# Routing of the first half in three pieces behind the last groups, and two splits of the shared expert moved ahead

## The chip, the core and the metric

One Trainium2 chip; the kernel runs on one of its cores. The metric is the device time of one execution in microseconds (us). Engines are TensorE (PE; PEld for its weight loads), VectorE (DVE), ScalarE (ACT), GpSimd (POOL) and SyncE (SP), which issues DMAs.

## The reference

x has 4096 rows of 128 values. Four sub-layers are applied one after the other, each to the layer norm of x, and each result is added to x:

```python
x = x + attn_a(layernorm(x))   # scores against 512 keys, (1 - arccos(s)/pi)**9, values, l2 norm
x = x + ffn(layernorm(x))      # layer 0 of the experts
x = x + attn_b(layernorm(x))   # linear attention, elu features, 16 heads
x = x + ffn(layernorm(x))      # layer 1 of the experts, same weights

# ffn
logits = xf @ gate_w + gate_b
top_w, top_i = top_k(logits, 2)
gw = softmax(top_w)
for e in range(8):
    h = gelu(xf @ w1[e] + b1[e])
    out = out + combine[:, e:e+1] * (h @ w2[e] + b2[e])
shared = gelu(xf @ ws1 + bs1) @ ws2 + bs2
```

## The kernel before

**Tiling.** The 4096 rows are 32 tiles of 128 rows, in NG = 8 groups of TPG = 4 tiles. A half is 4 groups (HT = 16 tiles). The routed experts work on units of 256 rows (39 of them per layer), the shared expert on NA = 16 half groups n (two for each group).

**Layer 0, first part.** Attention a ends with the value products. The parts of each engine are laid out by `by_units` (line 150), a list of (lag, part): at step n a part works on half group or group n - lag. On VectorE the list (line 1888) holds `third`, `ninth` (the ninth power), `first_add` (adds the values to x, and the moments of the gate's norm), `first_shift`, `first_hi` and `gate_lo` (the rows in two f16 halves) and `gate_logits`. TensorE's list is FIRST_ORDER (line 111): turn the gate rows, `value(g)` (line 1098), gate products. GpSimd computes one power per group for the values' norm (`x_scale`) and one for the gate's norm (`group_root`, recorded at line 671). ScalarE makes the squares of the values, the angles, the normalised rows and copies of turned rows.

**Layer 1, first part.** Linear attention. The lists are laid out by `straight` (line 97): LIN_ORDER (line 105) for TensorE, lists of their own on VectorE (line 1885) and ScalarE. `lin_add` (line 1636 in the trace) adds the projected result, then moments; `gate_shift` makes the shift of the gate's norm; `gate_lo` and `gate_logits` follow at lags 3 and 4.

**Routing.** `routing(half)` (line 1683) takes a half's logits on VectorE through 17 numbered steps: the two largest of 8 with their experts (lines 1703 to 1716, ending in PM, the mask of both), gates from a Tanh that ScalarE makes in `gap(half)` (GW, CB, lines 1719 to 1723), and places: TensorE counts with two products in `route(half)` (line 1219), and VectorE adds a scan over tiles (lines 1729 to 1756, ending in SLF, the row's place). `rows(g)` (line 1762) copies a group's rows, destinations, gates and places into one of 4 buffers (slot g % 4; it waits until the scatters of group g - 4 have landed). `gate_parts(half)` (line 1775) splits the gates in bf16 terms.

The first half's routing stands inside `gate_logits` right behind the logits of group 3:

```python
                    if g == NG // 2 - 1:
                        routing(0)
                        rows(0)
                    if NG // 2 <= g < NG - 1:
                        rows(g - NG // 2 + 1)
```

and on TensorE `route(0)` stands ahead of `value(NG - 1)` and of `lin_project(NG // 2 + 1)`.

**Scatters.** `scatter(g, ...)` (line 717, recorded at line 724) on GpSimd writes a group's rows to DRAM by place, 8 indirect DMAs a group, 64 a layer. In layer 0 the first group's 4 + 4 stand between the last powers, in layer 1 groups 0 and 1 (16) do. The others follow in `paced(g)` (line 736), each group behind a signal:

```python
                behind = {2: gates_done, 3: routing_done, 4: summed(1), 5: summed(2), 6: summed(4), 7: summed(5)}
```

**Shared expert.** TensorE's `shared_up` (n = 0 to 3 early), ScalarE's `shared_gelu`, VectorE's `shared_split` (lines 1808, 1810; splits the Gelu into f16 halves), TensorE's `shared_down` (ending in line 1270) and `shared_turn`, ScalarE's copy (line 1015), VectorE's `shared_add`. In VectorE's loop `later_rows` puts rows(5), (6), (7) ahead of the splits 1, 3, 6, `later_gates` gate_parts(1) at 4, and `later_table` the table of units behind split 7.

**Routed experts.** SyncE waits for the table, stores padding rows, waits for the first four groups' scatters, issues six transposing loads (line 561), then waits for all rows (`all_rows_stored`, line 546); tail loads (line 568, gate and destination of a unit's rows) come only behind that. TensorE multiplies up and down, VectorE splits (lines 1901, 1904) and makes the output (line 1915, `routed_out`, line 1907), ScalarE takes Gelu (line 1026) and the low part (line 1036, `routed_low`, line 1030, which needs the unit's tail), GpSimd scatters the results (line 778). Six units are in flight.

**PSUM.** Three rings of two banks, A, B and C, with counted turns (`USES`, LIN_RING, `lin_turns`, `route_bank`, line 393).

## Time and profile before

| what | us |
|---|---|
| median of 3 runs | 698.61 |
| lowest and highest | 694.57, 699.79 |
| profiled execution | 695.24 |
| its span | 693.4 |
| DVE busy | 552.1 (80%) |
| PE busy | 497.8 (72%) |
| ACT busy | 465.5 (67%) |
| POOL busy | 375.5 (54%) |

Positions such as "at 272.77" are microseconds from the start of the span. A timeline row has start, duration, engine, line, operation and tiles; in square brackets stands how long the engine was idle before it and what released it. "issue" means that the engine waited for nothing that the profile shows. An indirect DMA's row on POOL is the time in which GpSimd makes it; its landing comes later.

### The profile page before, as it was taken

How to read it: one execution, taken by the hardware profiler on the slowest of the kernel's cores; microseconds unless marked ns; L12 is line 12 of the kernel's file. 1: busy time of each engine (PE TensorE's matmuls, PEld its weight loads, DVE VectorE, ACT ScalarE, POOL GpSimd, SP SyncE). 2: the span in 40 equal slices, each digit the busy share in tenths (PEclk: the TensorE clock that was granted, in tenths of full speed). 3: DMA queues.
4: the chain of work that ended last, by engine and by line, in shares of the span. 5: the costliest groups of instructions: out<-in, count | busy, mean ns of one | idle time of the engine just before them, and what ended most of it. 6: DMA issues, size and time to landing. Idle time of an engine off the chain costs nothing.

```text
span 693.4 us, 14048 instructions
## 1 busy us (share of the span) xinstructions
PE 497.8 (72%) x3817; PEld 360.3 (52%) x3818; DVE 552.1 (80%) x1229; ACT 465.5 (67%) x937; POOL 375.5 (54%) x382
## 2 busy tenths in 40 slices
PE   1276725655456998999977678757569999999760
PEld 1132305555422446787866466646224469888650
DVE  4989666978668985899989778786679859998991
ACT  1379988998234665989966767845535569999750
POOL 5032201323477776677757722226677737777773
PEclk9999977968558999999999999967689999999996
DMA  8700000000011144444473310001111444545943
GB/s 277 215 8 0 1 0 0 1 1 0 16 47 47 52 115 81 91 98 100 104 194 85 96 35 1 1 9 36 39 48 57 115 80 94 100 101 137 228 112 125
DMA packets 95054, 51.12 MB, mean 74 GB/s; under 512 B 76026, under 2 KB 84180, under 8 KB 94996
## 3 DMA queue, kind: packets, MB, share of 16 engines
q1 hardware_dynamic: 85908, 31.67, 20.5%
q0 software_dynamic: 9088, 18.76, 9.0%
q8 instruction: 25, 0.41, 0.2%
q14 instruction: 33, 0.27, 0.1%
HBM read 16.27 MB, written 23.90 MB: 58 GB/s over the span
## 4 chain that ended last, share of the span: by engine, by line
PE 27%; DVE 21%; issue 17%; ACT 13%; POOL 11%; SPq 8%; DMA 3%; DVEq 0%; POOLq 0%; ACTq 0%
POOL routed_rows L724 8%; SPq L561 5%; PE PC L1107 5%; PE PC L1314 4%; DVE big L1901 2%; DMA RR<-expert_results 2%; DVE RR L1915 2%; ACT SC L834 2%; SPq L568 2%; ACT big L934 2%; PE PA L1125 2%; DVE big L1539 2%; PE PC L1316 2%; PE PA L1296 1%; PE PA L1298 1%
## 5 line engine op out<-in xcount | busy, mean ns | idle before, releaser
L778 POOL DMA_INDIRECT expert_results<-RR,DG x156 | 171.1, 1097 | 73.0 <-issue 45.9
L724 POOL DMA_INDIRECT routed_rows<-big,SLQ x128 | 137.5, 1074 | 56.1 <-issue 45.0
L1314 PE MATMUL PC<-W,big 128*128 x624 | 117.4, 275 | 25.9 <-DVE RR L1915 24.7
L1026 ACT ACTIVATE SC<-PA,B1T,scl 128x256 f32<-128x256 f32 x208 | 100.5, 571 | 21.6 <-PE PA L1298 12.2
L1904 DVE SCALAR_TENSOR_TENSOR big<-SC,scl,big 128x1024 f16<-128x1024 f32 x78 | 100.3, 1286 | 2.8
L1316 PE MATMUL PC<-W,big 128*128 x468 | 86.5, 221 | 0.0
L1314 PEld LDWEIGHTS PC<-W,big 128*128 128x128 f16 x624 | 57.9, 98 | 41.5 <-issue 36.8
L1107 PE MATMUL PC<-QW,big 128*128 128x128 f32 x256 | 42.7, 345 | 42.8 <-DVE big L1539 28.1
L1901 DVE TENSOR_SCALAR big<-SC,scl 128x1024 f16<-128x1024 f32 x78 | 65.1, 835 | 5.8 <-ACT SC L1026 5.8
L671 POOL TENSOR_TENSOR RS<-VA,halfneg 128x4 f32<-128x4 f32 x24 | 28.4, 1185 | 67.9 <-DVE VA L1573 67.8
L1107 PEld LDWEIGHTS PC<-QW,big 128*128 128x128 f32 x256 | 41.2, 257 | 45.0 <-DVE big L1539 29.4
L1036 ACT ACTIVATE big<-PC,DG 128x128 f32<-128x128 f32 x156 | 50.0, 386 | 18.3 <-PE PC L1314 13.9
L1296 PE MATMUL PA<-big,W1H 128*128 128x256 f16 x208 | 56.9, 274 | 1.0 <-DMA big<-routed_rows 0.7
L1026 ACT ACTIVATE SC<-PB,B1T,scl 128x256 f32<-128x256 f32 x104 | 50.6, 580 | 10.1 <-DVE big L1904 7.2
L1297 PE MATMUL PA<-big,W1H 128*128 128x256 f16 x208 | 56.9, 273 | 0.0
L1298 PE MATMUL PA<-big,W1L 128*128 128x256 f16 x208 | 56.8, 273 | 0.0
L903 ACT ACTIVATE SC<-PA,B1T,scl 128x512 f32<-128x512 f32 x64 | 45.8, 773 | 12.8 <-PE PA L1213 11.2
L1915 DVE SCALAR_TENSOR_TENSOR RR<-PC,DG,big 128x128 f32<-128x128 f32 x156 | 47.0, 344 | 8.8 <-ACT big L1036 8.0
L1316 PEld LDWEIGHTS PC<-W,big 128*128 128x128 f16 x468 | 46.0, 98 | 1.3
L1810 DVE SCALAR_TENSOR_TENSOR big<-SC,scl,big 128x1024 f16<-128x1024 f32 x32 | 41.1, 1285 | 1.1
L1086 PE MATMUL PA<-QT,KT 128*128 128x512 f32 x64 | 32.9, 638 | 12.7 <-DVE QT L1399 12.1
L1015 ACT ACTIVATE big<-PC,scl 128x512 f32<-128x512 f32 x16 | 11.0, 687 | 41.3 <-PE PC L1270 41.3
(284 smaller groups left out, 1268.3 us busy)
## 6 DMA issues: line engine op xcount, KB each, us to landing
RR<-expert_results SPq DMA_DIRECT2D x16, 512.0 KB, 4.2
routed_rows<-pad_zeros SPq DMA_DIRECT2D x23, 128.0 KB
expert_results<-RR,DG POOLq DMA_INDIRECT x156
X<-n_L_attn_a_hidden_states SPq DMA_DIRECT2D x2, 1024.0 KB, 6.5
big<-in_L_ffn_w SPq DMA_DIRECT2D x1, 2048.0 KB, 9.0
routed_rows<-big,SLQ POOLq DMA_INDIRECT x128, 2.4
out_x<-X SPq DMA_DIRECT2D x8, 256.0 KB
big<-routed_rows SPq DMA_TRANSPOSE x78
```

The source lines that it names most:

```text
L724: pool.indirect_dma_start(routed, bass.IndirectOffsetOnAxis(ap=SLQ[:, slot, t, c:c + 1], axis=0), XHL[:, slot, t, c, :].bitcast(I32), None ...
L778: pool.indirect_dma_start(results, bass.IndirectOffsetOnAxis(ap=DG[:, k, r, 0:1], axis=0), YT[:, k, r, :], None).then_inc(result_stored[k] ...
L1026: ins = act.activation(HF[:, k % 3, b * RU:(b + 1) * RU], up_out(k, b), ACT.Gelu, scale=INV1, bias=B1T[:, bass.ds(b1_at + b, 1)])
L1107: last = pe.matmul(PC[slot][:, t * D:(t + 1) * D], powers, QW[:, b, :], start=(b == 0), stop=(b == HB - 1))
L1296: pe.matmul(o, W1H[:, at], xh, start=True, stop=False)
L1297: pe.matmul(o, W1H[:, at], xl, start=False, stop=False)
L1298: last = pe.matmul(o, W1L[:, at], xh, start=False, stop=True)
L1314: last = pe.matmul(both, hh, W2[:, :, at], start=(b == 0), stop=(b == HB - 1))
L1316: pe.matmul(both[:, 0, :], hl, W2H[:, at], start=False, stop=False)
L1901: dve.tensor_scalar(HH3[:, k % 3, :], HF[:, k % 3, 0:HB * RU], SH, None, ALU.mult).then_inc(s["rhh_ready"], 1)
L1904: dve.scalar_tensor_tensor(HL3[:, k % 3, :], HF[:, k % 3, 0:HB * RU], SH, HH3[:, k % 3, :], ALU.mult, ALU.subtract).then_inc(s["rhl_ready" ...
L1915: ins = dve.scalar_tensor_tensor(YT[:, k, r, :], down_out(k)[:, r, 0, :], DG[:, k, r, 1:2].bitcast(F32), LOW[:, k % 2, r, :], ALU.mult, AL ...
```

## The change

The routing of a half is cut in three functions with the same instructions in another order: `choose(half)` (11 steps, to PM), `place(half)` (the places, to SLF) and `gates(half)` (GW, CB). Layer 0 places them at the ends of steps 16, 17 and 18 of VectorE's list, with rows(0) behind the gates, rows(1) and rows(2) two and four steps on, and gate_parts(0) behind rows(2). Layer 1 has `choose` at the end of step 8, `place` between the add and the shift of group 7 in step 9, gates and rows(0) at the end of step 9, and rows(1), rows(2) and gate_parts(0) in step 10. TensorE's `route(0)` stands behind the last values and the last projection, in layer 1 in ring A instead of C. GpSimd's scatters all stand behind the last root. For the second half, VectorE does `choose(1)`, the splits 0 and 1 of the shared expert, `place(1)`, `gates(1)`, rows(3) and rows(4). ScalarE makes `gap(1)` between the Gelus 1 and 2; in layer 1 `gap(0)` moves to step 9.

```diff
 def lin_turns(groups):
...
-                if (what, n - lag) == ("project", groups // 2 + 1):
+                t.take(what, n - lag, LIN_RING[what])
+                if (what, n - lag) == ("project", groups - 1):
                     for slot in range(2):
-                        t.take("route", slot, "C")
-                t.take(what, n - lag, LIN_RING[what])
+                        t.take("route", slot, LIN_RING["route"])
...
             if half == 0:
-                return PC[slot], c_read[slot], lin_free("route", slot)
+                return PA[slot], a_read[slot], lin_free("route", slot)
...
                 if layer:
 
-                    for n in range(NG):
-                        if n >= 2:
+                    for n in range(2, NG + 2):
+                        if n < NG:
                             group_root(n, 2)
-                        if n >= 2:
-                            if n == NG - 1:
-                                scatter(0, 0, 0, range(2))
-                            group_root(n - 2, 3)
-                    scatter(0, 0, 0, range(2, TPG))
-                    group_root(NG - 2, 3)
-                    scatter(1, 0, 1, range(2))
-                    group_root(NG - 1, 3)
-                    scatter(1, 0, 1, range(2, TPG))
-                    for g in range(2, NG):
-                        paced(g)
+                        group_root(n - 2, 3)
                 else:
-                    for g in range(NG - 2):
+                    for g in range(NG):
                         x_scale(g)
                         group_root(g, 1)
-                    x_scale(NG - 2)
-                    scatter(0, 0, 0, range(2))
-                    group_root(NG - 2, 1)
-                    x_scale(NG - 1)
-                    scatter(0, 0, 0, range(2, TPG))
-                    group_root(NG - 1, 1)
-                    scatter(1, 0, 1)
-                    for g in range(2, NG):
-                        paced(g)
+                for g in range(NG):
+                    paced(g)
...
                 def first_gap(g):
-                    if g == NG - 1:
+                    if g == 0:
                         gap(0)
...
-                                  (1, lin_exp_q), (0, first_gap), (0, lin_normalise), (0, lin_turn_x),
+                                  (1, lin_exp_q), (NG + 1, first_gap), (0, lin_normalise), (0, lin_turn_x),
...
-                gap(1)
                 for n in range(EARLY):
+                    if n == 2:
+                        gap(1)
                     shared_gelu(n, 0, n, early=True)
...
                 def gate_logits(g):
                     logits(g, g // 2, g % 2, "")
-                    if g == NG // 2 - 1:
-                        routing(0)
+
+                def first_routing(n):
+
+                    if n == 0:
+                        choose(0)
+                    if n == 1:
+                        place(0)
+                    if n == 2:
+                        gates(0)
                         rows(0)
-                    if NG // 2 <= g < NG - 1:
-                        rows(g - NG // 2 + 1)
+                    if n in (4, 6):
+                        rows(n // 2 - 1)
+                    if n == 6:
+                        gate_parts(0)
...
                 if layer:
                     straight(NG, [(0, lin_combine), (1, lin_elu_k), (4, gate_logits), (0, lin_shift), (3, gate_lo),
-                                  (1, lin_mask), (1, lin_elu_q), (2, lin_add), (1, lin_divide), (2, gate_shift)])
+                                  (NG + 2, lin_rows), (1, lin_mask), (1, lin_elu_q), (2, lin_add),
+                                  (NG + 1, lin_place), (1, lin_divide), (2, gate_shift), (NG, lin_choose),
+                                  (NG + 1, lin_gates)])
                 else:
                     by_units(NG, [(6, first_hi), (0, third, 1), (6, gate_lo), (4, first_shift), (8, gate_logits),
-                                  (1, ninth, 1), (3, first_add)])
-                routing(1)
+                                  (1, ninth, 1), (3, first_add), (2 * NG, first_routing, 1)])
+                choose(1)
+                wait(dve, s["rhl_ready"], layer * UNITS)
+                for n in range(2):
+                    shared_split(n, 0, n, early=True)
+                place(1)
+                gates(1)
+                rows(3)
                 rows(4)
-                gate_parts(0)
-                wait(dve, s["rhl_ready"], layer * UNITS)
```

## Rows read from the trace of the kernel before

**Rows 1.** The page, part 4: the chain that ended last, shares by line.

```profile
POOL routed_rows L724 8%; SPq L561 5%; PE PC L1107 5%; PE PC L1314 4%; DVE big L1901 2%; DMA RR<-expert_results 2%; DVE RR L1915 2%; ACT SC L834 2%; SPq L568 2%; ACT big L934 2%; PE PA L1125 2%; DVE big L1539 2%; PE PC L1316 2%; PE PA L1296 1%; PE PA L1298 1%
```

**Rows 2.** The chain that ended last, 270 to 279 us: start, us, what.

```profile
272.77 2.35 DMA routed_rows<-big,SLQ
...
275.37 0.42 SPq L568
...
277.74 0.42 SPq L568
```

**Rows 3.** Timeline of GpSimd (POOL), layer 0: start, us, instruction, idle before.

```profile
179.08 1.30 POOL L724 DMA_INDIRECT routed_rows<-big,SLQ  x1 [8.12 <-issue]
...
196.41 1.04 POOL L724 DMA_INDIRECT routed_rows<-big,SLQ  x1 [0.19 <-issue]
...
217.74 1.02 POOL L724 DMA_INDIRECT routed_rows<-big,SLQ  x1 [0.30 <-issue]
```

**Rows 4.** Timeline of GpSimd, layer 1.

```profile
495.29 1.00 POOL L724 DMA_INDIRECT routed_rows<-big,SLQ  x1 [1.55 <-PE PC L1196]
...
560.84 0.95 POOL L724 DMA_INDIRECT routed_rows<-big,SLQ  x1 [0.30 <-issue]
```

**Rows 5.** Busy us by engine in a stretch; then PE clock, DMA share, GB/s.

```profile
580.00:590.00 10.00, 10.00 (x110) 9.10 (x106) 9.86 (x17) 9.44 (x24) 7.55 (x9) 1.00 0.46 98
```

**Rows 6.** Timeline of VectorE (DVE), layer 0.

```profile
169.40 0.29 DVE L1703 TENSOR_REDUCE MX<-big 128x16 f32<-128x128 f32 x1
...
173.05 0.29 DVE L1716 TENSOR_TENSOR PM<-big 128x128 bf16<-128x128 f32 x1
...
174.40 0.17 DVE L1729 COPY D<-region_of 128x8 f32<-128x8 f32 x1
...
177.90 0.17 DVE L1772 CAST SLQ<-SLF 128x8 uint32<-128x8 f32 x1
...
189.97 1.13 DVE L1547 SCALAR_TENSOR_TENSOR X<-PC,RX,X 128x128 f32<-128x128 f32 x4 [1.25 <-POOL RX L671]
...
192.56 0.17 DVE L1573 TENSOR_SCALAR VA<-MV 128x4 f32<-128x4 f32 x1
```

**Rows 7.** Timeline of TensorE, the last two value groups.

```profile
164.38 3.84 PE L1107 MATMUL PC<-QW,big 128*128 128x128 f32 x32 [3.28 <-DVE big L1539]
...
180.39 6.77 PE L1107 MATMUL PC<-QW,big 128*128 128x128 f32 x32 [6.59 <-DVE big L1539]
```

**Rows 8.** Timelines of ScalarE (low parts of unit 1, both layers) and SyncE.

```profile
281.25 0.62 ACT L1036 ACTIVATE big<-PC,DG 128x128 f32<-128x128 f32 x2 [1.48 <-DMA DG<-routed_rows]
...
571.61 0.76 ACT L1036 ACTIVATE big<-PC,DG 128x128 f32<-128x128 f32 x2
...
565.93 0.42 SPq L568 DMA_DIRECT2D DG<-routed_rows  x1
```

**Rows 9.** Timeline of VectorE, layer 1.

```profile
454.89 0.28 DVE L1703 TENSOR_REDUCE MX<-big 128x16 f32<-128x128 f32 x1
...
463.42 0.17 DVE L1772 CAST SLQ<-SLF 128x8 uint32<-128x8 f32 x1
...
480.51 0.24 DVE L1678 SCALAR_TENSOR_TENSOR big<-PC,scl,GB 128x32 f32<-128x32 f32 x1
...
484.92 0.69 DVE L1636 TENSOR_TENSOR X<-PC,X 128x512 f32<-128x512 f32 x1 [0.92 <-PE PC L1172]
...
488.42 0.16 DVE L1579 SCALAR_TENSOR_TENSOR VB<-MV,RS 128x4 f32<-128x4 f32 x1 [1.16 <-POOL RS L671]
...
512.03 0.69 DVE L1766 COPY big<-PB 128x2048 f16<-128x2048 f16 x1
```

**Rows 10.** Timeline of ScalarE, layer 0: table load, first copied sum.

```profile
205.33 1.28 ACT L903 ACT_TABLE_LOAD   x1
...
222.42 0.69 ACT L1015 ACTIVATE big<-PC,scl 128x512 f32<-128x512 f32 x1 [7.85 <-PE PC L1270]
```

**Rows 11.** Instructions of line 724: duration in ns min, median, max.

```profile
L724 POOL DMA_INDIRECT routed_rows<-big,SLQ x128: 954/1016/1730, 179.1 to 560.8; - x128
```

More of the change, by code:

```diff
@@ L407, in lin_free @@
         def lin_free(what, g):
-            return used(LIN_RING.get(what, "C"), "linear", g % 2) + lin_turn[what, g]
+            return used(LIN_RING[what], "linear", g % 2) + lin_turn[what, g]
         def lin_read(what, g):
@@ L1109, in value @@
                 last.then_inc(s["o_ready"], 1)
+                if g == NG - 1:
+                    route(0)
             for layer in range(2):
@@ L1680, in logits, with route_step @@
                         GB[:].unsqueeze(1).to_broadcast([P, TPG, E]), ALU.mult, ALU.add).then_inc(c_read[k], 1)
[L1683 to L1687 removed]
+                def route_step(half, steps_before):
+                    n = [(2 * layer + half) * ROUTE_STEPS + steps_before]
                     def step(*several):
@@ L1716, in routing, with place @@
                     dve.tensor_tensor(PM[:, mine, :], OH[:, 0, :, :], OH[:, 1, :, :], ALU.add).then_inc(s["pm_ready"], 1)
-                    dve.wait_ge(s["th_ready"], done)
-                    step(*[dve.tensor_scalar(GW[:, mine, c], TH[:, mine], 0.5 - c, 0.5, ALU.mult, ALU.add)
-                           for c in range(2)])
-                    step(*[dve.tensor_tensor(CB2[:, c, :, :], OH[:, c, :, :], each(GW, c), ALU.mult)
-                           for c in range(2)])
-                    step(dve.tensor_tensor(CB[:, mine, 0:E], CB2[:, 0, :, :], CB2[:, 1, :, :], ALU.add))
+                def place(half):
+                    step, mine, done = route_step(half, CHOOSE_STEPS), half_tiles(half), 2 * layer + half + 1
                     dve.wait_ge(s["counts_ready"], done)
@@ L1799, in gate_parts, with shared_split @@
                     assert done[0] == (2 * layer + half + 1) * GATE_STEPS
-                def shared_split(n, h, k):
+                def shared_split(n, h, k, early=False):
+                    if isinstance(n, int) and n < 2 and not early:
+                        return
                     m, slot = layer * NA + n, k // 2
```

53 lines of the change are left out of this document (37 added, 16 removed).

## The prediction

> **What bounds the kernel now.** I read the chain that ended last first. Its largest entry by line is GpSimd's row scatter, L724, with 8%; SyncE's transposing loads, L561, come next with 5% [rows 1]. Where layer 0 turns from shared to routed experts the chain shows why: the last scatter is issued at 272.77, lands 2.35 us later, and the first tail load of the routed units goes at 275.37 [rows 2]. The routed stage waits for the last of 64 scatters. GpSimd's own timeline comes second. In layer 0, 8 scatters stand ahead of the last root. The other 56 run without a gap from 196.41 to 272.77, 76.36 / 55 = 1.39 us each [rows 2, 3]. In layer 1, 16 stand between the roots, and the other 48 start from 495.29 to 560.84, 65.55 / 47 = 1.39 us each [rows 4]. GpSimd is 54% busy over the span and yet ends this stage twice. Behind it VectorE sets the pace, 9.86 of 10 us busy in a stretch of the routed stage [rows 5], so what delays the first outputs delays the end.
>
> **The change, part by part.** All of it moves work; nothing on data is added or taken away. A part that leaves VectorE's path early is worth something only if the last scatter comes earlier.
>
> *(a) Routing leaves the middle, layer 0.* Routing and rows(0) stand on VectorE from 169.40 to 178.07, 8.67 us, ahead of the last two ninth powers [rows 6], and TensorE's last value group starts only at 180.39 [rows 7]. With them gone the ninth powers end, and the values start, at 180.39 - 8.67 = 171.7. The values take 3.84 us as in the group before or 6.77 as now [rows 7]: 175.5 or 178.5. Neither end decides, since VectorE does the sixth group's add and moments next (as in the last group, 189.97 to 192.73, 2.8 us [rows 6]), to 174.5, and then `choose`, 169.40 to 173.34 = 3.9 us, to 178.4.
>
> *(b) What comes back ahead of the last root, layer 0.* TensorE's two counting products now stand behind the last values, and the gate products of group 4 behind them: together 1.2 us after `choose`, which VectorE fills with hi and lo; `logits` ends at 180.1. Of the 3.67 us from 174.40 to 178.07 `place` is 2.6 and rows(0) 1.0: `place` ends at 182.7. The value squares on ScalarE now wait behind `gap(0)` until 177.3, but the root of the squares is there at about 181, under `place`: free, and 1 to 2 us if that cover went. Add and moments of the last group: 185.5 (now 192.73). `gates` 1.1 us (173.34 to 174.40) and rows(0) 1.0 give 187.6. The first scatter starts 1.0 us later (178.07 to 179.08 [rows 3, 6]), at 188.7.
>
> *(c) The scatters of layer 0.* None lies between roots any more: all 64 run from 188.7. The first sixteen of the long row start 1.33 us apart (196.41 to 217.74 [rows 3]), so 8 take 10.6 us, the ninth starts at 199.3 instead of 196.41 and the last at 275.7: **+2.9 us**. It is a loss although the last root comes some 8 us earlier, since 8 scatters were done in time that GpSimd had to spare. The pacing waits (gates, second routing, sums 1, 2, 4, 5) are met before their scatters. Nothing hides the 2.9: the low part of unit 1 at 281.25 already waits for its tail load [rows 8].
>
> *(d) The scatters of layer 1.* Routing and rows(0) stand from 454.89 to 463.59, 8.7 us; the last shift is at 488.42 [rows 9], and 8.7 less is 479.7. Back come `choose`, 3.9 us, of which some 3.6 fill the time to the last add (480.5 to 484.92 less logits and lo [rows 9]): +0.3; and `place`, 2.6, of which 1.16 fill the wait for the root: +1.4. Matmuls that were slow after the stall may speed up as in [rows 7], 0 to -2. Shift at 481.2, `gates` and rows(0) 2.2 us, first scatter 1.0 later: 484.4. All 64 run from there; 16 x 1.33 = 21.3 puts the 17th at 505.7, where it now starts at 495.29: **+10.4 us** on the last one (571.2). Here 16 scatters, not 8, lay in spare time.
>
> *(e) What the routed stage of layer 1 feels of it.* The tail load of unit 1 went at 565.93; such a load lands 3.5 us after its issue (layer 0: 277.74 to 281.25), and ScalarE used it at 571.61 [rows 2, 8], so 571.61 - 565.93 - 3.5 = 2.2 us are to spare. 10.4 - 2.2 = **+8.2 us**. TensorE's shared expert is not free of it either: rows(5), (6), (7) reuse the buffers of groups 1, 2, 3, so VectorE waits until scatters 16, 24 and 32 have landed, at about 509, 520 and 531. rows(6) stands at 512.03 now [rows 9]. Queued behind them are the splits from number 2, 3 and 6 on, and TensorE waits for those. I put its end some 4 us later than now (8 less what VectorE waits there today), still under the scatters: 0.
>
> *(f) The two early splits, and `gate_parts(0)` moved.* 4.0 us of splits go ahead of `place`, `gates` and rows(3), which come after. On VectorE it is a change of order. The first sum comes some 10 us earlier, and its reader, the pacing of the fifth group's scatters, isn't waiting. 0, hidden by the scatters.
>
> *(g) ScalarE's order.* `gap(1)` now stands between the second and third Gelu. The trace shows a load of 1.28 us between Tanh and Gelu [rows 10]; Tanh right after a Gelu it doesn't show. Loads both ways would be two more, 2.6 us a layer, and ScalarE sits idle for 7.85 us before its first copied sum [rows 10]: 0, at most +2.6 a layer without that cover. The Trainium skill, "ScalarE: Activation LUTs", section "Table sets: the hidden batching unit", has Tanh beside exp and arctan, Gelu in a set of its own, and says to batch calls by set, which speaks against this order. By it both loads come, and the sum stays as it is, since they lie under the scatters.
>
> *Sum:* 2.9 + 8.2 = 11.1 us. The profiled execution took 695.24 us (span 693.4), so 706.3 for it; the median of the runs, 698.61, lies 3.4 above it, and 698.6 + 11.1 = 709.7. I say **709 us**.
>
> *Bounds.* First scatters 187 to 191 and 482 to 487: -1.7 to +2.3 and -2.4 to +2.6. A scatter: 0.954 us at the least [rows 11] with 0.30 of issue, 1.26, to 1.39 as the mean now; for the added 8 and 16 that is -0.6 to +0.5 and -1.1 to +1.0. Spare time in (e) 0 to 3.1.
>
> **Rivals.**
> *A, the scatters run at their floor: not slower.* Single scatters take up to 1.730 us where the median is 1.016 [rows 11]. If VectorE's splits stretch them, a VectorE that sits in waits for rows(5) to (7) lets them run at 1.26. All at the floor: the last of layer 0 at 188.7 + 63 x 1.26 = 268.1, -4.7; of layer 1 at 484.4 + 79.4 = 563.8, +3.0 less 2.2 to spare, +0.8. Together -3.9: 694.7. It is no loss from a cadence of about 1.30 on. Against it: the mean is 1.39 in both layers, and the splits are as many as before. The Trainium skill, "SBUF — State Buffer", in its box on the "DVE blocks DMA" trap, says that a two-port operation of VectorE locks GpSimd out of writing descriptors. By it the long scatters are such locks and go with the splits.
> *B, layer 1 has more room.* The last groups gain more than in (d), the first scatter starts at 482, tails land in 2 us. Then layer 1 costs 10.4 - 2.4 - 1.5 - 1.1 (cadence) = 5.4, and layer 0 1.5: +7 and less. I put it at 4 to 7, 704.
> *C, the waits of rows(5) to (7) pass the scatters' end.* They hold splits, the table, and behind the table SyncE's pads and six transposes, and so the first routed unit. For: three waits of 5 to 8 us in layer 1. Against: today SyncE still waits for the last landing after its transposes. If they are through only at 577 instead of before the last landing at 573.7, the total is +15: 714.
>
> **Numbers.** Forecast 0.62 (706 to 712), B 0.18, A 0.12, C 0.08. The range takes in B and C and leaves A out: 701 to 716. A measurement of this kernel tells about 1%, 7 us, from no change. Slower by over 1%, above 705.6: the forecast, C and a sliver of B, 0.72. Within 1%: the rest of B and most of A, 0.23. Faster: the far end of A, 0.05.
>
> **What would show it.** After the change: no L724 ahead of the last root in either layer; first scatters at 189 and 487 (484.4 + 2.9), last ones at 276 and 574; the first outputs 3 and 11 us later; VectorE waiting 5 and 8 us before the rows copies of layer 1; table loads on both sides of the second Tanh. The prediction is wrong if the last scatter of layer 1 starts before 568, or if it starts at 574 and the outputs haven't moved.

## The result and the profile after

| | before | after |
|---|---|---|
| median of 4 runs of each | 697.06 | 719.35 (715.55 to 721.27) |
| ratio | | 1.033, 95% interval 1.028 to 1.037 |
| profiled execution, its span | 695.24, 693.4 | 718.17, 716.2 |

Slower by 3.3% where I had foretold 1.6%, and outside the range. The part of the page with the chain that ended last, after:

```profile
POOL routed_rows L724 13%; PE PC L1089 6%; SPq L561 5%; PE PC L1298 4%; SPq L568 2%; PE PA L1109 2%; DVE big L1934 2%; ACT big L917 2%; DMA RR<-expert_results 2%; DVE RR L1948 2%; DVE big L1523 2%; PE PC L1300 1%; PE PA L1070 1%; ACT SC L81
```

GpSimd's row scatter, 8% of the chain in [rows 1], is 13% now: the chain runs through it in both layers. In the kernel before it does so in layer 0 alone. Ahead of layer 1's first output its chain runs through TensorE, from the shared expert's products to the routed ones:

```profile
559.83 0.66 PE PC L1279 x4
560.49 0.20 PE PA L1296
```

GpSimd's timeline after, the last root, the first and the last scatter of layer 0, then of layer 1:

```profile
188.38 1.01 POOL L671 TENSOR_TENSOR RS<-VA,halfneg 128x4 f32<-128x4 f32 x1 [4.36 <-DVE VA L1557]
191.44 1.30 POOL L724 DMA_INDIRECT routed_rows<-big,SLQ  x1 [2.06 <-issue]
...
280.89 1.68 POOL L724 DMA_INDIRECT routed_rows<-big,SLQ  x1 [0.30 <-issue]
...
488.70 1.01 POOL L671 TENSOR_TENSOR RS<-VA,halfneg 128x4 f32<-128x4 f32 x1 [9.07 <-DVE VA L1557]
494.29 1.04 POOL L724 DMA_INDIRECT routed_rows<-big,SLQ  x1 [4.58 <-DVE SLQ L1797]
...
583.94 1.68 POOL L724 DMA_INDIRECT routed_rows<-big,SLQ  x1 [0.30 <-issue]
```

No scatter stands ahead of a root any more, and GpSimd idles 9.07 us in one piece before the last root of layer 1. The kernel before has made 12 scatters by its last root there, and 4 more follow ahead of [rows 4]:

```profile
487.34 1.04 POOL L671 TENSOR_TENSOR RS<-VA,halfneg 128x4 f32<-128x4 f32 x1 [2.09 <-DVE VA L1573]
488.58 1.03 POOL L724 DMA_INDIRECT routed_rows<-big,SLQ  x1 [0.20 <-issue]
```

After, the 63 intervals from first to last take 89.45 and 89.65 us. The next three fences are the first outputs: VectorE's rows before (layer 0, layer 1), VectorE's rows after, and SyncE's first tail loads after.

```profile
278.04 0.61 DVE L1915 SCALAR_TENSOR_TENSOR RR<-PC,DG,big 128x128 f32<-128x128 f32 x2 [1.12 <-ACT big L1036]
...
570.18 0.61 DVE L1915 SCALAR_TENSOR_TENSOR RR<-PC,DG,big 128x128 f32<-128x128 f32 x2
```

```profile
287.34 0.61 DVE L1948 SCALAR_TENSOR_TENSOR RR<-PC,DG,big 128x128 f32<-128x128 f32 x2 [3.62 <-ACT big L1020]
...
589.88 0.61 DVE L1948 SCALAR_TENSOR_TENSOR RR<-PC,DG,big 128x128 f32<-128x128 f32 x2 [3.10 <-ACT big L1020]
```

```profile
284.14 0.42 SPq L568 DMA_DIRECT2D DG<-routed_rows  x1
...
587.26 0.41 SPq L568 DMA_DIRECT2D DG<-routed_rows  x1
```

In layer 1 the first output came with no idle time ahead of it before; now VectorE waits 3.10 us, and the output stands 2.62 us behind the tail load.

All positions are best counted from a point ahead of the change: VectorE's logits of group 3, which start at 169.06 and 454.55 before and at 171.65 and 463.80 after. "Last" is the start of the last scatter, "slow" the number of scatters of over 1.5 us in a layer, all from the timelines:

| kernel, layer | first scatter | last | first output | slow |
|---|---|---|---|---|
| before, 0 | 10.0 | 103.7 | 109.0 | 4 |
| after, 0 | 19.8 | 109.2 | 115.7 | 9 |
| before, 1 | 9.9 | 106.3 | 115.6 | 4 |
| after, 1 | 30.5 | 120.1 | 126.1 | 10 |

The 22.8 us between the spans are: 2.6 ahead of the logits of group 3 in layer 0, where both kernels have the same instructions; 6.7 to the first output of layer 0; nothing from there to the logits of layer 1 (176.5 in both); 10.5 to the first output of layer 1; and 3.1 from that output to the end (123.2 before, 126.3 after). For this last piece see the stretches after; the first two are of layer 0, the others of layer 1, columns as in [rows 5]:

```profile
284.00:288.00 4.00, 1.32 (x13) 0.94 (x10) 0.66 (x3) 1.42 (x4) 0.00 (x0) 1.00 0.23 38
288.00:292.00 4.00, 3.81 (x25) 3.03 (x26) 3.93 (x6) 3.94 (x11) 2.94 (x2) 0.57 0.33 67
...
588.00:590.00 2.00, 0.37 (x4) 0.09 (x1) 0.12 (x1) 0.78 (x3) 0.00 (x0) 1.00 0.29 49
...
592.00:594.00 2.00, 2.00 (x12) 1.47 (x11) 1.94 (x5) 2.00 (x6) 1.70 (x2) 0.50 0.45 91
594.00:596.00 2.00, 2.00 (x17) 1.56 (x16) 2.00 (x4) 1.34 (x5) 1.64 (x2) 0.69 0.52 104
```

TensorE has run out of units that it may work ahead: it is busy 1.32 of 4 us behind the landing of the last scatter (283.9) in layer 0, and 0.37 of 2 us in layer 1. Then its granted clock is 0.57 and 0.50, which is the lower of its two levels (1.2 of 2.4 GHz) for most or all of the stretch, just when the first outputs are wanted; before, it was 1.00 throughout both places.

### The profile page after: what moved, and what is told of

Its sections match the earlier page's. It is cut to its first block, busy times and chain, and to the rows that moved or that the text cites. A ratio compares the mean times of both kernels' runs of the same rounds, so it can differ in the third digit from the quotient of the medians.

```text
span 716.2 us, 14044 instructions
## 1 busy us (share of the span) xinstructions
PE 507.0 (71%) x3817; PEld 366.1 (51%) x3818; DVE 551.2 (77%) x1229; ACT 467.0 (65%) x937; POOL 383.2 (54%) x382
## 3 DMA queue, kind: packets, MB, share of 16 engines
q1 hardware_dynamic: 85908, 31.67, 19.6%
## 4 chain that ended last, share of the span: by engine, by line
PE 25%; DVE 18%; issue 16%; POOL 15%; ACT 12%; SPq 9%; DMA 3%; DVEq 0%; POOLq 0%; ACTq 0%
POOL routed_rows L724 13%; PE PC L1089 6%; SPq L561 5%; PE PC L1298 4%; SPq L568 2%; PE PA L1109 2%; DVE big L1934 2%; ACT big L917 2%; DMA RR<-expert_results 2%; DVE RR L1948 2%; DVE big L1523 2%; PE PC L1300 1%; PE PA L1070 1%; ACT SC L817 1%; SPq L559 1%
## 5 line engine op out<-in xcount | busy, mean ns | idle before, releaser
L724 POOL DMA_INDIRECT routed_rows<-big,SLQ x128 | 144.1, 1126 | 45.0 <-issue 39.2
L1298 PE MATMUL PC<-W,big 128*128 x624 | 120.3, 279 | 32.1 <-DVE RR L1948 31.1
L1010 ACT ACTIVATE SC<-PA,B1T,scl 128x256 f32<-128x256 f32 x208 | 100.6, 569 | 23.0 <-DVE big L1937 11.1
L1937 DVE SCALAR_TENSOR_TENSOR big<-SC,scl,big 128x1024 f16<-128x1024 f32 x78 | 100.2, 1285 | 2.8
L1300 PE MATMUL PC<-W,big 128*128 x468 | 88.4, 223 | 0.0
L1298 PEld LDWEIGHTS PC<-W,big 128*128 128x128 f16 x624 | 58.9, 100 | 46.8 <-issue 41.6
L1089 PE MATMUL PC<-QW,big 128*128 128x128 f32 x256 | 46.6, 367 | 36.4 <-DVE big L1523 21.6
L1934 DVE TENSOR_SCALAR big<-SC,scl 128x1024 f16<-128x1024 f32 x78 | 63.4, 812 | 5.9 <-ACT SC L1010 5.9
L1089 PEld LDWEIGHTS PC<-QW,big 128*128 128x128 f32 x256 | 45.1, 278 | 38.4 <-DVE big L1523 22.9
L1010 ACT ACTIVATE SC<-PB,B1T,scl 128x256 f32<-128x256 f32 x104 | 50.4, 571 | 13.3 <-DVE big L1937 11.4
L1280 PE MATMUL PA<-big,W1H 128*128 128x256 f16 x208 | 57.8, 278 | 0.2
L1281 PE MATMUL PA<-big,W1H 128*128 128x256 f16 x208 | 57.7, 277 | 0.0
L1250 PE MATMUL PC<-big,W 128*128 128x512 f16 x64 | 28.0, 437 | 34.0 <-DVE big L1837 24.7
L1300 PEld LDWEIGHTS PC<-W,big 128*128 128x128 f16 x468 | 46.8, 100 | 1.5
```

The lines of the kernel that those rows point to most:

```text
L724: pool.indirect_dma_start(routed, bass.IndirectOffsetOnAxis(ap=SLQ[:, slot, t, c:c + 1], axis=0), XHL[:, slot, t, c, :].bitcast(I32), None ...
L1010: ins = act.activation(HF[:, k % 3, b * RU:(b + 1) * RU], up_out(k, b), ACT.Gelu, scale=INV1, bias=B1T[:, bass.ds(b1_at + b, 1)])
L1089: last = pe.matmul(PC[slot][:, t * D:(t + 1) * D], powers, QW[:, b, :], start=(b == 0), stop=(b == HB - 1))
L1280: pe.matmul(o, W1H[:, at], xh, start=True, stop=False)
L1281: pe.matmul(o, W1H[:, at], xl, start=False, stop=False)
L1298: last = pe.matmul(both, hh, W2[:, :, at], start=(b == 0), stop=(b == HB - 1))
```

## The experiments

Each kernel was compared with the kernel before on the same chip; ratios are to that, with 95% intervals. The change and its parts are rebuilt by two switches per layer: where the first half's routing stands, and in which order the second half goes.

**Layers and halves.** `only_layer0` has the change in layer 0 and the old places in layer 1, `only_layer1` the reverse; `first_half_only` moves the first half's routing and the scatters in both layers, `second_half_only` the rest.

```diff
+MID = (False, True)       # first half's routing where it was: only_layer0
+PLAIN = (False, True)     # second half's order as it was
...
-                for g in range(NG):
+                for g in range(2 if MID[layer] else 0, NG):
                     paced(g)
```

> The whole change in layer 0 alone; layer 1 in the order of before. Theory S (the scatters that lay in GpSimd's spare time, 8 in layer 0 and 16 in layer 1, are moved behind the last root, and the routed stage waits for the last scatter): layer 0 carries its own part only, +5 to +7 us on the time of before, last scatter of layer 0 some 5 us later, nothing in layer 1 beyond that. Rival O (the loss is in the order of the second half: splits ahead of place, gates and rows): the same +5 to +7 here, so this run does not part the two. Rival X (the layers feed each other, a later start of layer 1 costs more than itself): under +3 or over +10.

> The whole change in layer 1 alone; layer 0 in the order of before. Theory S: +13 to +16 us, with the last scatter of layer 1 some 14 us later than before counted from the logits of group 3, and the first output of the routed stage 10 us later. Rival X: clearly less or more than the 22.3 us of the change less what the run of layer 0 alone shows.

> First half's routing in three pieces and all scatters behind the last root, second half in the order of before. Theory S: nearly the whole loss, +18 to +24 us. Rival O: +12 us or less.

> First half's routing where it was (mid stage, scatters between the roots), only the second half reordered: two splits ahead of place and gates, Tanh between Gelus 1 and 2. Theory S: no scatter leaves spare time, so -1 to +3 us (the scatter cadence may shift a little). Rival O: most of the loss, +10 us or more.

Measured: 1.0137 (1.0062 to 1.0212), 1.0230 (1.0157 to 1.0302), 1.0297 (1.0226 to 1.0368) and 1.0077 (1.0042 to 1.0112). The loss is in both layers, and nearly all of it in the first half. That layer 1 has more of it is told by the positions above (10.5 us at the first output for 6.7); the intervals of the two ratios overlap. The last scatter stands where the change has it in each layer that carries the change (110.2 in layer 0 of `only_layer0`, 119.7 in layer 1 of `only_layer1`) and where the kernel before has it in the other (106.5, 103.8). The second half's 0.8% was more than I gave it; its own controls come below.

**The spare time between the roots.** `roots_first` is the kernel before, with routing untouched and only GpSimd's order changed.

```diff
-                    x_scale(NG - 2)
-                    scatter(0, 0, 0, range(2))
-                    group_root(NG - 2, 1)
...
+                    for g in range(NG):
+                        x_scale(g)
+                        group_root(g, 1)
+                    for g in range(NG):
+                        paced(g)
```

> The kernel before, with nothing changed but GpSimd's order: in both layers all scatters stand behind the last root, so the 8 scatters of layer 0 and the 16 of layer 1 that lay between the powers lose their place. Theory (the scatters set the end of this stage, and the change lost the time that GpSimd had to spare): the last root of layer 0 comes some 2 us earlier (about 193 instead of 195.2), all 64 scatters run from about 194.5 at 1.42 us each, and the last one starts near 284 (+10 to +11). In layer 1 the last one starts near 577 plus the delay of layer 0 (+16), of which 4 us are to spare (tail load to first output, 6.6 us before, 2.6 after), so +12 at the outputs. Together +20 to +24 us, ratio 1.030 to 1.035, as much as the whole change. Rival 1 (the roots were held up by the scatters ahead of them, so both orders are worth the same): at most +6 us, ratio under 1.01. Rival 2 (the longer cadence of the change comes from its own second half or early routing): here the mean row of L724 stays at 1.07 to 1.08 us with 4 or 5 rows over 1.5 us a layer; by my theory it rises to 1.12 to 1.14 with 9 to 11 rows over 1.5, since VectorE then waits in rows(5) to rows(7) and the splits start in step with landings.

Measured: 1.0408 (1.0360 to 1.0455), 28 us, more than I expected. From the logits of group 3 the last scatter starts at 113.5 and 124.0 (before 103.7 and 106.3), 63 intervals take 89.8 and 90.0 us, and 11 scatters a layer are slow. So the lost places alone cost more than the whole change, and the later routing gives part of it back. The longer cadence isn't made by the new place of routing either: it came with the kernel before, as soon as all 64 stood behind the root.

**One step earlier.** Layer 0 and the second halves as before; in layer 1 the pieces of the change stand one step earlier, with 4 scatters ahead of the last root.

```diff
-                                  (NG + 1, lin_place), (1, lin_divide), (2, gate_shift), (NG, lin_choose),
-                                  (NG + 1, lin_gates)])
+                                  (NG, lin_place), (1, lin_divide), (2, gate_shift), (NG - 1, lin_choose),
+                                  (NG, lin_gates)])
...
+                        if n == NG + 1:
+                            scatter(0, 0, 0, range(2))
                         group_root(n - 2, 3)
```

> Layer 0 and both second halves in the order of before. In layer 1 the three pieces of the first half stand one step earlier than in the change (choose at the end of step 7, place, gates and rows(0) in step 8, rows(1), rows(2) in step 9, route(0) behind the projection of group 6), and 4 of the scatters go ahead of the last root. Theory (it is the spare time between the roots that the change lost): the first scatter comes 5 to 8 us earlier against the logits of group 3 (23 to 26 us behind them instead of 30.5), four scatters cost nothing, and the last one stands 114 to 117 us behind the logits instead of 120; the outputs follow, TensorE doesn't fall to the lower clock at their start or does so for less long, and the time is 706 to 709 us on the scale of 697 before, ratio 1.012 to 1.018, against 1.0230 for layer 1 as the change has it. So it still loses to the kernel before, which puts 16 there. Rival (the pieces in step 7 and 8 delay the groups behind them by what they bring): last scatter 119 us or more behind the logits, ratio 1.020 or more.

Measured: 1.0129 (1.0076 to 1.0183), in the range foretold. The first scatter starts 26.3 us behind the logits of group 3 and the last 117.3, at the far end of what was foretold. But the logits of group 7 are at 39.7 us, as before (39.9), where the change has them at 34.0: in steps 7 and 8 the pieces delay the last groups by what they bring. A scatter in spare time is paid for with routing in the middle, and the kernel before, with 12 of them ahead of the last root of layer 1, gains by it.

**What a split does to a scatter.** After, GpSimd's and VectorE's timelines over the same stretch of layer 0:

```profile
224.35 0.96 POOL L724 DMA_INDIRECT routed_rows<-big,SLQ  x1 [0.30 <-issue]
225.62 1.65 POOL L724 DMA_INDIRECT routed_rows<-big,SLQ  x1 [0.30 <-issue]
227.57 1.73 POOL L724 DMA_INDIRECT routed_rows<-big,SLQ  x1 [0.30 <-issue]
229.61 1.68 POOL L724 DMA_INDIRECT routed_rows<-big,SLQ  x1 [0.30 <-issue]
231.59 1.02 POOL L724 DMA_INDIRECT routed_rows<-big,SLQ  x1 [0.30 <-issue]
```

```profile
225.51 0.69 DVE L1791 COPY big<-PB 128x2048 f16<-128x2048 f16 x1 [7.35 <-DMA routed_rows<-big,SLQ]
...
227.18 1.28 DVE L1837 SCALAR_TENSOR_TENSOR big<-SC,scl,big 128x1024 f16<-128x1024 f32 x1
228.38 0.75 DVE L1835 TENSOR_SCALAR big<-SC,scl 128x1024 f16<-128x1024 f32 x1
229.17 1.28 DVE L1837 SCALAR_TENSOR_TENSOR big<-SC,scl,big 128x1024 f16<-128x1024 f32 x1
```

The scatters of 227.57 and 229.61 start 0.39 and 0.44 us behind the start of a split's second operation (L1837, 1.28 us) and take 1.73 and 1.68 us; with nothing beside them they take 0.96. A slow scatter and its issue are 2.04 us, two operations of a split 1.99, so splits that stand back to back can hit one scatter after the other. `after_no_low` and `before_no_low` cut that operation, from split 4 on, to 16 of its 1024 columns (8 of 512 in each of two blocks; the expectations give it as 8 of 256 a tile).

```diff
-                    dve.scalar_tensor_tensor(HL[:, slot, b, :], hf, SH, HH[:, slot, b, :], ALU.mult,
-                                             ALU.subtract).then_inc(s["hl_ready"], 1)
+                    all_ = isinstance(n, int) and n < 4
+                    few = slice(0, GT if all_ else 8)
+                    dve.scalar_tensor_tensor(HL[:, slot, b, few], hf[:, :, few], SH, HH[:, slot, b, few], ALU.mult,
+                                             ALU.subtract).then_inc(s["hl_ready"], 1)
```

> The changed kernel; from split 4 of the shared expert on, the second operation of a split (the low f16 half, 1.28 us on VectorE, L1837) works on 8 columns of each tile instead of 256, so that part of the low halves is left out of the product. Theory (a scatter issued under that operation is held until it has ended: 1.68 to 1.73 us instead of 0.96): rows of L724 over 1.5 us fall from 9 and 10 a layer to at most 3 and the mean row from 1.12 to about 1.03; the last scatter stands 82 to 85 us behind the first instead of 89.5. As the scatters set the end of the stage in both layers, the time falls by 5 to 6 us in layer 0 and 4 to 6 in layer 1, to 707 to 711, ratio to the kernel before 1.015 to 1.022. Rival (the slow scatters come from queue or DMA traffic, or from any VectorE work): mean row and distance stay within 1.5 us of the changed kernel's, and so does the time (ratio 1.029 to 1.034), although VectorE has 24 x 1.2 = 29 us less to do.

> The kernel before with the same cut (second operation of the splits 4 to 15 on 8 columns of each tile; part of the low halves is left out). Theory: few scatters were slow here (4 a layer over 1.5 us), so the last scatter comes 3 to 4 us earlier in each layer; layer 0 gives that to the end, layer 1 has its outputs set by other work (6.6 us from tail load to first output), so nothing there: 3 to 4 us, ratio 0.994 to 0.996. The difference between the changed kernel and the one before, both without the low halves, is then 14 to 19 us instead of 22.7: what the cadence added goes, the lost time between the powers stays. Rival (the cadence has no part in the loss): the difference stays at 22 us or more.

Measured: 1.0208 (1.0159 to 1.0257) and 0.9938 (0.9906 to 0.9970). The same two engines in layer 0 of `after_no_low`:

```profile
250.72 0.23 DVE L1839 SCALAR_TENSOR_TENSOR big<-SC,scl,big 128x16 f16<-128x16 f32 x1
...
251.59 0.98 DVE L1835 TENSOR_SCALAR big<-SC,scl 128x1024 f16<-128x1024 f32 x1
252.60 0.23 DVE L1839 SCALAR_TENSOR_TENSOR big<-SC,scl,big 128x16 f16<-128x16 f32 x1
```

```profile
249.64 1.17 POOL L724 DMA_INDIRECT routed_rows<-big,SLQ  x1 [0.31 <-issue]
251.11 0.96 POOL L724 DMA_INDIRECT routed_rows<-big,SLQ  x1 [0.30 <-issue]
252.38 1.01 POOL L724 DMA_INDIRECT routed_rows<-big,SLQ  x1 [0.30 <-issue]
```

The scatters that meet the short operation take 1.17 and 1.01 us. First to last scatter fell from 89.45 and 89.65 us to 86.3 and 87.6; 6 and 8 slow ones are left, more than the 3 foretold, since the four whole splits, the routed ones at the end and the row copies still hit. The time fell with it, by 1.2% of 697, 8 us, and the outputs went with the scatters: behind the logits of group 3 the last scatter of `after_no_low` starts 3.2 and 1.3 us earlier than after, the first output comes 3.7 and 1.1 us earlier. The cut also takes work off VectorE (29 us by the expectation), so the 8 us are not the scatters' alone. Without the low halves the two kernels differ by 1.0208 - 0.9938 = 2.7%, 19 us, for 3.3% with them. By that some 4 us of the loss are cadence and the rest is not, but the intervals, some 0.5% each way, don't part 2.7 from 3.3.

**Why more scatters are slow.** My theory was that VectorE's waits for landed scatters in rows(5) to (7), new with the change, put its splits in step with GpSimd, as in the fence above behind a wait of 7.35 us.

```diff
-                rows_at = {1: 5, 3: 6, 6: 7}
+                rows_at = {4: 5, 6: 6, 7: 7}      # rows_later
+                rows_at = {4: 5, 8: 6, 11: 7}     # no_row_waits, with VectorE's loop written out
```

> The changed kernel; rows(5), (6) and (7) stand ahead of the splits 4, 6 and 7 of the shared expert instead of 1, 3 and 6, so that VectorE waits less for landed scatters (14.3 us in layer 0 and 17.1 us in layer 1 now), and its splits don't start together with a scatter that follows a landing. Theory (the waits bring splits and scatters in step, and bunch the splits): waits under 9 us a layer, rows of L724 over 1.5 us fall from 9 and 10 to 4 to 6 a layer, the mean row from 1.12 to 1.08, first to last scatter from 89.5 to 86.5 or 87 us, and the time by 4 to 6 us, ratio to the kernel before 1.024 to 1.027. Rival (every split under a scatter costs the same, wherever it stands, and the wait does nothing): slow rows, distance and ratio as in the change (9 to 11, 89.5, 1.030 to 1.035).

> The changed kernel; VectorE's loop of the shared expert is written out, so that rows(5), (6) and (7) can stand ahead of the splits 4, 8 and 11, by when the scatters that they wait for have landed (in rows_later the waits were only moved: 10.7 and 16.0 us were left). Same work, same number of scatters. Theory (the waits put VectorE's splits in step with the scatters): under 3 us of waits for landings a layer, 4 to 6 rows of L724 over 1.5 us a layer instead of 9 and 10, mean row 1.08, first to last scatter 86.5 to 87.5 us instead of 89.5, time 4 to 6 us less, ratio to the kernel before 1.024 to 1.027. Rival (splits cost scatters the same in any place): 9 or more slow rows a layer, 89 us or more, ratio 1.030 to 1.035.

`rows_later` gave 1.0323 (1.0245 to 1.0401), 10 and 15 slow scatters, but it left waits of 10.7 and 16.0 us, so it told nothing apart. In `no_row_waits` the kernel before took 803 us beside it, over 100 more than in the comparisons above: 1.0005 (0.9918 to 1.0093) says nothing on this case. A second one of it:

> The kernel of no_row_waits again, since there the kernel before took 803 us too, 100 more than in every other comparison, with VectorE idle in stretches that wait for nothing. Theory (VectorE's waits for landings put its splits in step with the scatters): under 5 us of waits for landings a layer, 4 to 6 rows of L724 over 1.5 us a layer, first to last scatter 86.5 to 87.5 us instead of 89.5, ratio to the kernel before 1.024 to 1.027. Rival (splits cost scatters the same in any place): 9 or more slow rows a layer, 89 us or more, ratio 1.030 to 1.035.

It had the kernel before at 801 us (ratio 0.9960, 0.9900 to 1.0020), so it says nothing either. A third one:

> The kernel of no_row_waits a third time, as the kernel before took 801 us in the second comparison too. There the waits for landings were gone in layer 0 and 4.7 us in layer 1, and yet 9 and 10 rows of L724 were over 1.5 us. If that holds where the kernel before takes 697 us, my theory of the waits falls: 9 or more slow rows a layer, first to last scatter 89 us or more, ratio 1.030 to 1.040. If the disturbed stretches made it, 4 to 6 slow rows, 86.5 to 87.5 us, and 1.024 to 1.027.

Measured with the kernel before at 696: 1.0310 (1.0240 to 1.0379). VectorE's waits in layer 1, first in the changed kernel, then here:

```profile
DVE big L1791 <- DMA routed_rows<-big,SLQ: 17.1, 3, 7.4
DVE X L1845 <- PE PC L1263: 3.9, 2, 3.8
```

```profile
DVE RR L1952 <- ACT big L1020: 16.7, 1, 16.7
DVE X L1845 <- PE PC L1263: 3.9, 2, 3.8
DVE big L1791 <- DMA routed_rows<-big,SLQ: 3.7, 1, 3.7
```

The waits for landed scatters are down from 17.1 us to 3.7 in layer 1, and from 14.3 to 0.6 in layer 0. Yet 10 scatters a layer are slow (one of them at 1.50 us), and first to last takes 92.0 and 89.9 us. My theory falls. The second fence says more: VectorE is through with the shared expert sooner and then stands 16.7 us before the first output, which is where it was (125.9 us behind the logits of group 3 for 126.1), as is the last scatter (120.4 for 120.1). VectorE's own work isn't what holds that output.

What the profiles bear out is a count. In the kernel before, 17 and 16 second operations lie between first and last scatter, and in 4 of them a layer a scatter starts in the first half of the operation; after, 18 and 18, with 7 and 8 hit. These are all the slow scatters of the kernel before, and all but two a layer of those after. The other two (225.62 and 238.43 in layer 0) start 0.1 us behind the copy of a group's rows (L1791) that had waited for a landed scatter, so that much of my theory is in the trace. In all layers with the old order 3 to 8 scatters are slow, in all with 64 behind the root 9 to 15 (kernels without the low halves and the comparisons at 800 us left out). What sets the phase is open.

**The second half.** Here both layers have the first half as before. `three_pieces_in_place` only makes the places ahead of the gates; `gap_between_gelus` has the later Tanh besides, `splits_ahead` the two early splits.

```diff
                 choose(1)
+                wait(dve, s["rhl_ready"], layer * UNITS)     # splits_ahead
+                for n in range(2):
+                    shared_split(n, 0, n, early=True)
                 place(1)
                 gates(1)
...
                 for n in range(EARLY):
+                    if n == 2:                               # gap_between_gelus
+                        gap(1)
                     shared_gelu(n, 0, n, early=True)
```

> Routing of the first half and the scatters as before in both layers; of the second half only ScalarE's order changes: gap(1), the Tanh, between the Gelus 1 and 2 instead of ahead of Gelu 0 (VectorE: choose, place, gates, rows(3), rows(4), no split ahead). My prediction cost this at 0. The whole second half alone measured 1.0077 [1.0042, 1.0112], so some 5 us lie in it. Theory (it is the wait for the Tanh): gates(1), rows(3) and rows(4) come some 4 us later, the splits behind them too, and the ratio is 1.004 to 1.008. Rival (the early splits cost it, by standing ahead of place, and so do the waits of rows for landed scatters): 1.000 +- 0.003 here. No table load between Gelu and Tanh or back in either case, as none is in the trace of the changed kernel.

> Routing of the first half and the scatters as before in both layers; of the second half only VectorE's order changes: the splits 0 and 1 ahead of place(1), gates(1), rows(3) and rows(4); ScalarE's gap(1) stays ahead of the Gelus. Theory: rows(3) and rows(4) come 4 us later but are wanted by no scatter yet (group 3's is due some 30 us on), so 1.000 to 1.003. Rival (this order is what costs): 1.005 to 1.008, with the last scatter 1 to 3 us later against the logits of group 3 and more rows of L724 over 1.5 us than 4 a layer.

> The control of the last three kernels: routing cut in choose, place and gates but left where it was in both layers and both halves, scatters, Tanhs and splits as before; all that differs from the kernel before is that VectorE makes the places ahead of the gates instead of behind them. Theory: 1.000 +- 0.003; then the later Tanh costs 0.4% and the early splits 1.0% by themselves. Rival (the order of the pieces costs by itself, since the Tanh comes under place): 1.003 to 1.005; then the later Tanh is free, as I predicted, and the early splits cost 0.5 to 0.6%.

Measured: 1.0044 (1.0014 to 1.0075), 1.0098 (1.0067 to 1.0130) and, for the control, 1.0070 (1.0039 to 1.0101). The first lies in the range that I had given to the Tanh, but the control, which leaves the Tanh where it was, took no less, so the later Tanh isn't shown to cost anything. The early splits come to 0.3% against the control, within the intervals. They aren't shown to be free either: in layer 1 of `splits_ahead` 8 scatters are slow, the last one starts at 110.0 (control 107.4, before 106.3) and the first output stands at 116.9 (115.5 and 115.6), which is the rival's sign. What costs even with neither is the order of the pieces, which I had not costed as an edit. From PM to the last row of rows(0) VectorE takes 4.85 us before (173.05 to 177.90 [rows 6]) and 5.33 in the control, 4.92 and 5.99 in the second half of layer 0, since the gates no longer fill the wait for TensorE's counts. In layer 1 the two halves take 0.4 and 0.5 us more, 2.5 over all four. Behind the logits of group 3 its profiled execution is 2.0 us longer than that of before, but that of `gap_between_gelus`, with the same order of pieces, is 1.7 us shorter. So where the 0.7% (4.9 us) come from stays open.

**Two scatters moved into idle time.** `fewer_between` is the kernel before with two scatters of layer 0 moved into the 3.33 us in which GpSimd idled before x_scale(7).

```diff
                     group_root(NG - 2, 1)
+                    scatter(0, 0, 0, range(2, 3))
                     x_scale(NG - 1)
-                    scatter(0, 0, 0, range(2, TPG))
+                    scatter(0, 0, 0, range(3, TPG))
```

> The kernel before; in layer 0 two of the four scatters that stand between x_scale(7) and the last root go ahead of x_scale(7), where GpSimd is idle for 3.3 us (185.2 to 188.6). Theory (the last root waits for the scatters ahead of it, 192.7 to 195.2, and the scatters set the end): last root at about 193.0, the 9th scatter at 194.2 instead of 196.4, the last one 2.2 us earlier, and so the end: 696.9 for 699.1, ratio 0.997, which five rounds may just tell. Rival (roots and scatters are not what binds): 1.000 +- 0.002, with the last scatter where it was against the logits of group 3.

Measured: 0.9982 (0.9951 to 1.0013). GpSimd's timeline around the last root:

```profile
186.76 0.96 POOL L724 DMA_INDIRECT routed_rows<-big,SLQ  x1 [0.30 <-issue]
188.54 0.23 POOL L706 TENSOR_SCALAR RX<-SS 128x4 f32<-128x4 f32 x1 [0.82 <-ACT junk L887]
...
192.79 1.14 POOL L671 TENSOR_TENSOR RS<-VA,halfneg 128x4 f32<-128x4 f32 x1 [0.33 <-DVE VA L1574]
194.13 1.03 POOL L724 DMA_INDIRECT routed_rows<-big,SLQ  x1 [0.20 <-issue]
```

The ninth scatter starts at 194.13 and the last one 101.2 us behind the logits of group 3, 2.5 earlier, as the theory had it. Its median is the lower one (695.3 for 696.8), but its interval takes in no change, so it isn't shown to be faster.

## Why the prediction was wrong

The mechanism was right in the main: the change slows the kernel because scatters lose GpSimd's spare time, in both layers, and more in layer 1. What failed is the size of the cadence term in (c) and (d), and what was put at nothing: the last scatter's own length and all that follows the first output.

*What bounds the kernel.* Two readings were off and changed no term. In layer 1 of the kernel before the chain didn't run through the scatters, so "ends this stage twice" was true of layer 0 only; (e) allowed for it with its time to spare. And of the 16 scatters "between the roots" 12 are, as shown above; the sum went by the 17th, which was read rightly.

*(a), (b) held.* The first scatter of layer 0 was put at 188.7, 19.6 us behind the logits of group 3; measured 19.8. In layer 1 29.9 was foretold, 30.5 measured.

*(c) and (d), the cadence, failed.* The sum gave the scatters that moved 1.33 us each and let the rest of the row keep its 1.39: the last scatter was to be as late as the ninth in layer 0 and the seventeenth in layer 1. That makes 87.0 and 86.8 us for the 63 intervals; measured 89.45 and 89.65. The moved scatters were priced nearly right: the first 8 intervals of layer 0 took 10.7 us for 10.6, the first 16 of layer 1 22.1 for 21.3. It was the rest of the row, taken over unchanged, that grew: its 55 intervals from 76.4 to 78.8 us, 1.43 each, and its 47 from 65.6 to 67.5, 1.44 each. The row had moved against VectorE's splits, and they hit it nearly twice as often. Together that is 2.5 and 2.8 us. The last scatter itself took 1.68 us for 1.02, so its landing came another 0.6 to 0.7 late. The Trainium skill, "SBUF — State Buffer", section "SBUF: two separate sides", box on the "DVE blocks DMA" trap, names a lock of GpSimd by VectorE's two-port operations; I used it only for rival A, that scatters may get faster. The trace agrees in kind (0.96 us alone, 1.68 to 1.73 behind a started second operation), though the operation here is one with two input tiles, and it worked the other way: no row ran at rival A's 1.26.

*(c), "Nothing hides the 2.9", held,* and the first output was later by more than the last scatter: 6.7 for 5.5, of which some 0.65 is the later landing.

*(e) was half right.* 10.4 with 2.2 to spare gave 8.2. Measured 13.85 on the last scatter and 10.5 at the first output: 4.0 to spare (from first tail load to first output 6.6 us before, 2.6 after), less 0.6 for the later landing. That room is rival B's in part. But the text stopped at the first output. From there to the end the change takes 3.1 us more. What goes with it: TensorE idles before the late output and then runs at the lower clock (592 to 596), and VectorE's waits for loads of results grew from 11.4 to 13.0 us. In `only_layer1`, `first_half_only`, `after_no_low` and `roots_first` too the first 20 us behind that output have a mean clock of 0.91; in `only_layer0`, `second_half_only`, `before_no_low` and `fewer_between` it is 1.00, as before. But the clock isn't shown to be the cause. Layer 0 has the same 0.91 after and loses nothing from its first output to the logits of layer 1, and `one_step_earlier` has 1.00 and yet takes 126.2 us from there to the end, `second_half_only` 125.1. How the 3.1 us divide stays open. VectorE's waits in rows(5) to rows(7) came as foretold (17.1 us in layer 1) and cost nothing: `no_row_waits_4`, nearly without them, is no faster. So rival C fell.

*(f) and (g).* The later Tanh isn't seen to cost anything, and no table load came with it. ScalarE, layer 1, after:

```profile
496.51 1.28 ACT L886 ACT_TABLE_LOAD   x1
499.76 2.79 ACT L886 ACTIVATE SC<-PA,B1T,scl 128x512 f32<-128x512 f32 x4 [1.96 <-PE PA L1197]
502.43 0.22 ACT L953 ACTIVATE TH<-DD 128x16 f32<-128x16 f32 x1
503.78 1.45 ACT L886 ACTIVATE SC<-PA,B1T,scl 128x512 f32<-128x512 f32 x2 [1.13 <-PE PA L1197]
```

The one load stands ahead of the Gelus; the Tanh at 502.43 runs between them and needs none. The Trainium skill, "ScalarE: Activation LUTs", section "Table sets: the hidden batching unit", put the two in different sets; the trace doesn't bear that out. What (f) overlooked is that gates behind places is an edit as well: 0.7% by its control (0.4 to 1.0%), 2.5 us of VectorE's time by the timelines.

*The sum.* By the spans, the code's share is 22.8 - 2.6 = 20.2 us for 11.1 foretold. The 2.6 are not the change's: TensorE's value groups ahead of the logits of group 3 take 3.84 us at the higher clock and up to 6.8 otherwise, three of them 3.84 in the profile before and one after:

```profile
135.03 6.79 PE L1089 MATMUL PC<-QW,big 128*128 128x128 f32 x32 [2.99 <-DVE big L1523]
...
166.98 3.84 PE L1089 MATMUL PC<-QW,big 128*128 128x128 f32 x32 [3.29 <-DVE big L1523]
```

Of the 9.1 us between 20.2 and 11.1, 5.3 are cadence, 1.3 the last scatter's own length and 3.1 the time behind the first output, less 1.8 that layer 1 had to spare above my 2.2; the other terms held within 1 us each.

## What to carry to other kernels

When work of an in-order engine moves out of its spare time, price the whole row anew, and not only what was added: here the added scatters cost what was foretold, and those behind them, moved against their neighbour's work, got slower. Where that turns on how two streams meet, give the mean spacing a wide range (1.39 us a scatter before, 1.42 to 1.47 in the kernels with all 64 in one row). Follow a late end past its first reader: here TensorE came back from its wait at the lower clock. And when a block is cut into pieces, their new order is an edit of its own and wants its own control.

## What the runs showed that I had not expected

- Scatters and splits beat: 1.99 us for a split's two operations, 2.04 for a slow scatter and its issue, so once one is hit, the next can be too (227.57 and 229.61 above). With VectorE's waits taken away the count stayed at 10 a layer.
- In one comparison both kernels took 803 us, and in the next some 801. In `no_row_waits` VectorE stood up to 30.8 us in one piece there, released by nothing on its own core that the profile shows; why is open. The 3% between the kernels vanished (1.0005 and 0.9960), so the level of the kernel before is to be looked at ahead of any ratio.
- Identical instructions ahead of the change differ between profiled executions by several us: the logits of group 3 start between 167.8 and 175.4 in the kernels above. A difference of spans under 1% needs a point ahead of the change to count from.
